# Gated scan and mixture of experts: the router's second layer by column quarters, with new engine orders

## The chip, the cores and the metric

The kernel runs on one core of a Trainium2 chip. The metric is the device time of one execution in microseconds, the median of the timed runs. The profile is of one more execution of the same program, taken by the hardware profiler; times from it are given from the start of its span.

## What is computed

The input is 2 x 2048 tokens of 128 numbers. The first half is a gated linear scan over time, the second a mixture of eight experts, of which each token takes the two best:

```python
h = _layernorm(x, axis=-1) * (1 + ca) + sa
x = x + ga * _L0_attn_ref(h, ...)        # gates, a linear scan along the 2048 tokens
h = _layernorm(x, axis=-1) * (1 + cb) + sb
# the second half, for each token of h:
logits = silu(h @ rw1 + rb1)             # 128 -> 512, the first router layer
logits = logits @ rw2 + rb2              # 512 -> 8, the second router layer
k_logits, k_index = jax.lax.top_k(logits, 2)
k_prob = softmax(k_logits)
# the sum over the two experts e of a token: k_prob * (silu(h @ w1[e] + b1[e]) @ w2[e] + b2[e])
```

All is float32. sa, ca, ga, sb, cb and gb come from a small product of silu(c) with wmod.

## The kernel before, in words

The 4096 tokens are cut into eight groups of 512 (G), four to each sequence. Each group g passes through these parts, and each part is a function in the code, named as in the plan:

- stats1, norm1 (VectorE, L630 to L647) and rstd1 (GpSimd, L450): the first layer norm. turn_x (TensorE, L930), modulate (ScalarE, L525), gates (TensorE, L977 and L978), tanh, decay, clamp, mult (ScalarE, L533 to L553), input (VectorE, L699) and scan (VectorE, L706 and L711): the scan over time, each group after the one before.
- turn_y (TensorE) and resid (VectorE, L716, with the second layer norm's statistics), rstd2 (GpSimd, L475), norm2 (VectorE, L725 and L730), turn_h (TensorE), copy (ScalarE, L559), dup (ScalarE, L563).
- router n (TensorE, L1001): a quarter h of the first router layer for group g, n = 4 g + h. silu n (ScalarE, L572) writes it to SBUF, hidden units on the partitions and 512 tokens along them. It alternates between banks 2 and 3, so router n + 2 waits for silu n.
- logits g (TensorE, L1015): the second router layer, with the activations standing and the eight columns of weights streamed, for each of four token tiles four products that add up in PSUM.
- top2 g (VectorE, L736 to L753) adds the second bias, finds the two best experts and their masks. share g (ScalarE, L577) makes the probabilities. rank g (TensorE, L1024 and L1027) counts the tokens ahead of each in its expert, place g (VectorE, L760 to L769) makes each token's slot.
- send n (GpSimd, L483): four indirect DMAs that write two token tiles, two copies each, to the sorted rows in HBM. There are sixteen sends, 64 DMAs.

After group 3, count:0 and table1 make the table of the first nine expert tiles (EARLY), which SyncE may load (L375) when the first half's dispatches have landed. After group 7, count:1 and table2 make the rest; SyncE first writes padding behind each expert's rows (L364, eight DMAs, which wait for pad_i from table2), then waits for the table, for the padding and for the second half's dispatches, and loads tile 9 onward.

An expert tile s is 256 rows of one expert, 39 tiles in all: tx (turn, L1041), xT (VectorE, L864), l1 (L1052), hid (ScalarE, L585), l2 (L1065), yb (L594), ty (L1073), sc (VectorE, L890), scat (GpSimd, L492, two indirect DMAs), with w1 and w2 (VectorE, L873 and L882) copying the expert's weights. From tile 12 on these run in a loop with a fixed order.

Each engine runs its parts strictly in the order in which its list in PLAN names them, and every part waits on semaphores for what it reads and for the buffers that it overwrites. Of the old lists the parts that matter here are:

```python
"vector": ... norm2:2 top2:0 norm1:6 place:0 input:4 input:5 scan:4 norm2:3 top2:1 stats1:7 place:1 resid:4 scan:5
          ... top2:7 w2:3 sc:1 place:7 xT:5 w1:5 sc:2 w2:4 w2:5 xT:6 w1:6 sc:3 table2:0
"scalar": ... silu:4 dup:0 dup:1 tanh:5 silu:5 copy:2 silu:6 share:0 silu:7 decay:5
"gpsimd": ident:0 rstd1:0 const:0 wsel:0 rstd1:1 ... rstd1:5 rstd2:0 rstd2:1 rstd2:2 rstd1:6
          rstd2:3 send:0 send:1 rstd1:7 send:2 rstd2:4 send:3 rstd2:5 send:4 send:5 rstd2:6 send:6 send:7 rstd2:7 send:8 ...
```

## Time and profile before

| what | value |
|---|---|
| median of 3 timed runs | 314.01 us |
| lowest and highest | 312.12, 314.21 us |
| span of the profiled execution | 344.7 us (the page gives no other time for it) |
| granted TensorE clock, mean over the span | 0.880 |
| TensorE, VectorE, ScalarE, GpSimd busy | 79%, 57%, 50%, 48% |

Times of the profile are of that one execution and run from its first instruction. "PE" is TensorE's products, "PEld" its weight loads, "DVE" VectorE, "ACT" ScalarE, "POOL" GpSimd, "SP" SyncE; a line such as L1015 is a line of the kernel. A float32 product is recorded as two weight loads and two matmuls.

### The profile page before, as it was taken

The page shows a single profiled execution, that of the slowest core. Times are in us where ns is not written, and L with a number is a line of the kernel's source. Part 1 is how long each engine was busy: PE and PEld are TensorE (multiplying, and loading weights), DVE is VectorE, ACT ScalarE, POOL GpSimd, SP SyncE. Part 2 cuts the span into 40 slices and gives each one's busy share as a digit, 9 for nine tenths or more (in the row PEclk, how much of TensorE's full clock was granted, in tenths as well). Part 3 has the DMA queues.
Part 4 walks back from the last instruction along what each step waited for, and adds up shares of the span by engine and source line. Part 5 has one row for each costly group of instructions (what it writes and reads, how often), then busy time and mean ns, then how long its engine had stood idle before and what let it go on. Part 6 is the DMA issues. An engine that isn't in the chain of part 4 may idle for free.

```text
span 344.7 us, 5139 instructions
## 1 busy us (share of the span) xinstructions
PE 273.9 (79%) x1290; PEld 208.6 (61%) x1290; DVE 196.8 (57%) x730; ACT 172.6 (50%) x327; POOL 164.5 (48%) x181
## 2 busy tenths in 40 slices
PE   0877598996978856999934799999999999999400
PEld 0543246664546444868823578888888888888300
DVE  4989899876967643544450234444434444447626
ACT  1079988796867403532400444555555554555100
POOL 4322013378668471547575344544555445555700
PEclk9999698788797876986996699999999999999955
DMA  8990000011111151101122353222222365002366
GB/s 232 321 276 0 0 2 2 8 57 39 40 46 42 54 142 29 33 32 54 42 77 77 92 136 96 70 60 55 62 72 76 84 172 156 19 23 67 92 186 179
DMA packets 41080, 28.43 MB, mean 82 GB/s; under 512 B 4895, under 2 KB 37713, under 8 KB 41056
## 3 DMA queue, kind: packets, MB, share of 16 engines
q1 hardware_dynamic: 34034, 18.60, 20.1%
q0 software_dynamic: 4544, 8.47, 7.5%
q10 hardware_dynamic: 2478, 1.09, 1.2%
q8 instruction: 9, 0.15, 0.2%
q14 instruction: 15, 0.12, 0.1%
HBM read 16.39 MB, written 12.67 MB: 84 GB/s over the span
## 4 chain that ended last, share of the span: by engine, by line
PE 58%; DVE 14%; another core or an unknown queue 9%; ACT 8%; issue 5%; DMA 3%; POOL 1%; DVEq 1%; SPq 0%; POOLq 0%; ACTq 0%
PE bank L1052 20%; PE bank L1065 16%; PE bank L1001 7%; PE bank L1015 4%; PE bank L1041 3%; PE bank L1073 2%; PE bank L977 2%; PE bank L930 2%; PE bank L978 2%; DVE st L630 2%; DMA av<-expert_out 1%; ACT hT L525 1%; ACT hT L585 1%; DVE rows L725 1%
## 5 line engine op out<-in xcount | busy, mean ns | idle before, releaser
L492 POOL DMA_INDIRECT expert_out<-shared,tx x78 | 78.0, 1000 | 73.1 <-DVE shared L890 59.7
L585 ACT ACTIVATE hT<-bank,w_t 128x256 f32<-128x256 f32 x156 | 65.2, 471 | 45.5 <-PE bank L1052 26.1
L483 POOL DMA_INDIRECT sorted_rows<-rows,sloti x64 | 65.3, 1021 | 41.4 <-DVE sloti L769 23.8
L1052 PE MATMUL bank<-xT,w_t 128*128 128x256 f32 x312 | 79.8, 402 | 0.0
L1065 PE MATMUL bank<-hT,w_t 128*128 128x256 f32 x312 | 75.8, 387 | 0.1
L1052 PEld LDWEIGHTS bank<-xT,w_t 128*128 128x128 f32 x312 | 60.8, 204 | 8.9 <-issue 1.2
L1065 PEld LDWEIGHTS bank<-hT,w_t 128*128 128x128 f32 x312 | 57.8, 196 | 6.8 <-DVE w_t L882 0.3
L1001 PE MATMUL bank<-h2T,rw_s 128*128 128x512 f32 x64 | 41.5, 752 | 7.8 <-issue 3.9
L594 ACT ACTIVATE yT<-bank,w_t 128x256 f32<-128x256 f32 x39 | 18.5, 474 | 49.9 <-PE bank L1065 32.0
L864 DVE COPY xT<-bank 128x256 f32<-128x256 f32 x39 | 16.5, 424 | 39.3 <-PE bank L1041 21.8
L873 DVE COPY w_t<-w_s 128x516 f32 x39 | 17.2, 440 | 25.0 <-issue 13.9
L890 DVE TENSOR_TENSOR shared<-bank,tx 128x256 f32<-128x256 f32 x39 | 16.5, 424 | 25.9 <-PE bank L1073 21.6
L1041 PE MATMUL bank<-ident,tx 128*128 128x128 f32 x78 | 15.9, 287 | 14.1 <-DVE xT L864 7.9
L882 DVE COPY w_t<-w_s 128x513 f32 x39 | 17.2, 442 | 15.8 <-issue 12.7
L1073 PE MATMUL bank<-ident,yT 128*128 128x128 f32 x78 | 15.9, 286 | 8.7 <-issue 7.5
L475 POOL TENSOR_TENSOR rs<-ve,half_neg 128x4 f32<-128x4 f32 x8 | 8.7, 1087 | 28.9 <-DVE ve L635 28.8
L1041 PEld LDWEIGHTS bank<-ident,tx 128*128 128x128 f32 x78 | 11.0, 151 | 18.9 <-issue 15.8
L1001 PEld LDWEIGHTS bank<-h2T,rw_s 128*128 128x128 f32 x64 | 12.0, 225 | 13.7 <-issue 5.6
L1073 PEld LDWEIGHTS bank<-ident,yT 128*128 128x128 f32 x78 | 11.0, 147 | 14.8 <-issue 9.5
L977 PE MATMUL bank<-hT,wx_bd 128*128 128x512 f32 x16 | 12.8, 896 | 6.3 <-ACT hT L525 6.3
L450 POOL TENSOR_TENSOR rs<-ve,half_neg 128x4 f32<-128x4 f32 x8 | 8.2, 1026 | 19.0 <-DVE ve L635 19.0
L1015 PEld LDWEIGHTS bank<-rw_s,qv 128*128 128x128 f32 x128 | 15.9, 204 | 1.7 <-issue 1.0
(176 smaller groups left out, 354.6 us busy)
## 6 DMA issues: line engine op xcount, KB each, us to landing
tx<-sorted_rows SPq DMA_DIRECT2D x39, 130.0 KB
w_s<-in_L_ffn_w_dram SPq DMA_DIRECT2D x16, 256.0 KB, 6.2
xs<-in_L_attn_x_dram SPq DMA_DIRECT2D x8, 256.0 KB, 5.2
av<-expert_out SPq DMA_DIRECT2D x8, 256.0 KB, 3.8
qv<-expert_out SPq DMA_DIRECT2D x8, 256.0 KB, 5.4
expert_out<-shared,tx POOLq DMA_INDIRECT x78
sorted_rows<-padr SPq DMA_DIRECT2D x9, 130.0 KB
sorted_rows<-rows,sloti POOLq DMA_INDIRECT x64
```

Source lines behind the costliest of these rows:

```text
L483: p.indirect_dma_start(sorted_rows[:, :], bass.IndirectOffsetOnAxis(ap=sloti[:, k, t:t + 1], axis=0), rows[:, t, k, :], None).then_inc(s_d ...
L492: p.indirect_dma_start(expert_out[:, :], bass.IndirectOffsetOnAxis(ap=xr_i[:, s % U, n, D + 1:D + 2], axis=0), yo[:, s % U, n, :], None, b ...
L585: ins = nc.scalar.activation(hsT[:, u % 2, h, :], bank[4 + q][:, (h % 2) * SL:(h % 2 + 1) * SL], ACT.Silu, bias=w1_t[:, u % 2, HID + h:HID ...
L594: nc.scalar.activation(yT[:, u % 2, :], bank[7][:, 0:SL], ACT.Identity, bias=w2_t[:, u % 2, HC * D:W2E]).then_inc(s_yT_e, 1)
L873: v.tensor_copy(w1_t[:, u % 2, :], w1_s[:, bass.ds(e * WE, WE)]).then_inc(s_w1t, 1)
L977: t.matmul(bank[z][:, :], wx_bd[:, :], hT[:, cols(g)], start=True, stop=True)
L1001: t.matmul(bank[2 + n % 2][:, :], rw1_s[:, h * P:(h + 1) * P], h2T[:, g % 2, :], start=True, stop=True).then_inc(s_rl1, 1)
L1015: ins = t.matmul(bank[6][:, j * NE:(j + 1) * NE], hr[g % 2][:, h, j * P:(j + 1) * P], rw2_s[:, h, :], start=(h == 0), stop=(h == HC - 1))
L1041: ins = t.transpose(bank[1][:, n * P:(n + 1) * P], xr[:, u, n, 0:D], ident[:, :])
L1052: ins = t.matmul(bank[4 + h // 2][:, (h % 2) * SL:(h % 2 + 1) * SL], w1_t[:, u % 2, h * P:(h + 1) * P], xT[:, u % 2, :], start=True, stop= ...
L1065: ins = t.matmul(bank[7][:, 0:SL], w2_t[:, u % 2, h * D:(h + 1) * D], hsT[:, u % 2, h, :], start=(h == 0), stop=(h == HC - 1))
L1073: ins = t.transpose(bank[1][:, n * P:(n + 1) * P], yT[:, u % 2, n * P:(n + 1) * P], ident[:, :])
```

## The change

The second router layer is computed the other way round. The weights stand: for each quarter h of the hidden units, 128 x 32 columns of which eight are used and 24 are zero (rw2_q). The activations are streamed, 512 columns. Each quarter writes its own 32 partitions of bank 6, and nothing is added up in PSUM (logits). A new ScalarE part, lgq, copies the bank to SBUF and adds the second bias, which stands on the first eight partitions (rb2_c). A new TensorE part, fold, multiplies the four token tiles of that copy with a 128 x 8 matrix of four stacked unit matrices (fold), which adds the quarters and turns the result. top2 reads the logits from PSUM; its bias addition goes, and so does the product that spread the bias. The logits, ranks and counts move between banks 6 and 7. VectorE builds the two new constants in consts. All four lists of PLAN are new. In the diff below the old lists are left out.

```diff
+        rw2_q = sb("rw2_q", [P, HC, P // HC])
+        rb2_c = sb("rb2_c", [P, 1])
+        fold = sb("fold", [P, NE])
+        lgq = sb("lgq", [P, G])
...
-        ones_row = sb("ones_row", [1, P])
...
-        lg = sb("lg", [P, GT, NE])
...
-        rb2_row = sb("rb2_row", [1, NE])
-        rb2_b = sb("rb2_b", [P, NE])
...
+        def logit_bank(g):
+            return bank[7 if g < GPB else 6][:, 0:GT * NE]
+
         def rank_bank(g):
-            return bank[7][:, 0:GT * NE] if g < GPB else bank[6][:, GT * NE:2 * GT * NE]
-
-        def counted():
-            return bank[6][:, 2 * GT * NE:2 * GT * NE + NE]
+            return bank[7 if g < GPB else 6][:, GT * NE:2 * GT * NE]
+
+        def counted(n):
+            return bank[7 - n][:, 2 * GT * NE:2 * GT * NE + NE]
...
             "tensor": """
+                turnc:0 turnb:0 mod:0 turn_x:0 gates:0 modrow:0 turn_x:1 turn_x:2 turn_x:3 gates:1 gates:2
+                gates:3 turn_y:0 turn_x:4 turn_x:5 gates:4 turn_h:0 turn_y:1 gates:5 turn_y:2 turn_y:3
+                router:0 router:1 router:2 router:3 turn_h:1 logits:0 router:4 fold:0 turn_x:6 router:5
+                router:6 router:7 turn_h:2 gates:6 rank:0 router:8 router:9 logits:1 turn_h:3 turn_y:4 fold:1
+                router:10 router:11 turn_y:5 router:12 router:13 router:14 rank:1 logits:2 turn_x:7 router:15
+                fold:2 gates:7 turn_y:6 rank:2 logits:3 turn_h:4 fold:3 router:16 router:17 turn_h:5 rank:3
+                router:18 router:19 turn_y:7 count:0 logits:4 router:20 router:21 turn_h:6 fold:4 router:22
+                router:23 router:24 rank:4 turn_h:7 router:25 router:26 logits:5 router:27 fold:5 router:28
+                router:29 router:30 rank:5 router:31 logits:6 tx:0 tx:1 l1:0 fold:6 l1:1 tx:2 l2:0 tx:3 l2:1
+                ty:0 rank:6 l1:2 ty:1 logits:7 tx:4 l1:3 l2:2 tx:5 fold:7 l2:3 l1:4 rank:7 tx:6 l1:5 ty:2
+                count:1 l2:4 l1:6 l2:5 ty:3 ty:4 l2:6 tx:7 tx:8 l1:7 ty:5 l1:8 ty:6 l2:7 tx:9 ty:7 l2:8 tx:10
+                l1:9 ty:8 l1:10 tx:11 l2:9 tx:12 l1:11 ty:9 l2:10""",
             "vector": """
+                stats1:0 setup:0 stats1:1 setup2:0 norm1:0 csilb:0 soft:0 mods:0 stats1:2 stats1:3 colsb:0
+                norm1:1 norm1:2 norm1:3 stats1:4 stats1:5 input:0 scan:0 rowsA:0 norm1:4 norm1:5 resid:0
+                consts:0 input:1 norm2:0 input:2 input:3 scan:1 scan:2 scan:3 resid:1 resid:2 norm2:1 resid:3
+                stats1:6 stats1:7 norm1:6 norm2:2 top2:0 input:4 scan:4 norm2:3 place:0 input:5 input:6 scan:5
+                top2:1 norm1:7 resid:4 resid:5 norm2:4 place:1 scan:6 top2:2 place:2 resid:6 norm2:5 top2:3
+                input:7 scan:7 place:3 resid:7 norm2:6 norm2:7 top2:4 place:4 table1:0 table1b:0 w1:0 w1:1
+                top2:5 place:5 w2:0 xT:0 xT:1 rowsB:0 w1:2 top2:6 xT:2 w2:1 w2:2 xT:3 w1:3 place:6 sc:0 sc:1
+                xT:4 w1:4 w1:5 w2:3 top2:7 xT:5 w2:4 w2:5 xT:6 w1:6 place:7 sc:2 table2:0 w2:6 sc:3 sc:4 w2:7
+                w1:7 xT:7 xT:8 w2:8 w1:8 w1:9 sc:5 sc:6 xT:9 sc:7 w2:9 w1:10 xT:10 sc:8 w2:10 xT:11 w1:11
+                w1:12 xT:12 w2:11 sc:9""",
             "scalar": """
+                ecs:0 esp:0 modulate:0 tanh:0 decay:0 clamp:0 modulate:1 mult:0 modulate:2 modulate:3 tanh:1
+                decay:1 tanh:2 tanh:3 decay:2 decay:3 modulate:4 clamp:1 clamp:2 modulate:5 mult:1 mult:2
+                clamp:3 mult:3 tanh:4 copy:0 decay:4 clamp:4 mult:4 silu:0 silu:1 tanh:5 silu:2 silu:3 copy:1
+                decay:5 lgq:0 clamp:5 silu:4 silu:5 silu:6 modulate:6 dup:0 copy:2 silu:7 tanh:6 silu:8 silu:9
+                dup:1 share:0 mult:5 lgq:1 copy:3 decay:6 silu:10 silu:11 dup:2 silu:12 clamp:6 mult:6 share:1
+                silu:13 silu:14 lgq:2 dup:3 dup:4 modulate:7 silu:15 share:2 tanh:7 decay:7 lgq:3 copy:4
+                clamp:7 mult:7 silu:16 silu:17 share:3 copy:5 silu:18 silu:19 lgq:4 silu:20 silu:21 copy:6
+                silu:22 share:4 silu:23 silu:24 silu:25 silu:26 dup:5 dup:6 copy:7 dup:7 lgq:5 silu:27 silu:28
+                silu:29 share:5 lgq:6 hid:0 hid:1 silu:30 share:6 yb:0 yb:1 silu:31 hid:2 lgq:7 hid:3 yb:2
+                share:7 yb:3 hid:4 hid:5 yb:4 hid:6 yb:5 yb:6 hid:7 hid:8 yb:7 yb:8 hid:9 hid:10 yb:9 hid:11""",
             "gpsimd": """
+                ident:0 const:0 wsel:0 rstd1:0 rstd1:1 rstd1:2 rstd1:3 rstd1:4 rstd1:5 rstd2:0 rstd2:1 rstd2:2
+                rstd1:6 rstd1:7 rstd2:3 send:0 rstd2:4 rstd2:5 send:1 send:2 send:3 send:4 rstd2:6 rstd2:7
+                send:5 send:6 send:7 send:8 send:9 send:10 send:11 send:12 send:13 send:14 send:15 scat:0
+                scat:1 scat:2 scat:3 scat:4 scat:5 scat:6 scat:7 scat:8 scat:9 scat:10 scat:11 scat:12""",
...
...
                 sp.dma_start(xs[:, tiles(g), :], x_t[:, tiles(g), :]).then_inc(s_x[g], 16)
             sp.dma_start(rw1_s[:, :], rw1).then_inc(s_rw, 16)
             sp.dma_start(rw2_s[:, :, :], rw2.rearrange("(c p) e -> p c e", p=P)).then_inc(s_rw, 16)
-            sp.dma_start(rb2_row[:, :], rb2.rearrange("(a e) -> a e", a=1)).then_inc(s_rw, 16)
+            sp.wait_ge(s_zero, 2)
+            sp.dma_start(rb2_c[0:NE, :], rb2.rearrange("(e a) -> e a", a=1)).then_inc(s_rw, 16)
             for g in range(GPB, NG):
                 sp.dma_start(xs[:, tiles(g), :], x_t[:, tiles(g), :]).then_inc(s_x[g], 16)
             for e in range(NE):
...
             def identity(_):
                 p.memset(ident[:, :], 0.0).then_inc(s_zero, 1)
+                p.memset(rb2_c[:, :], 0.0).then_inc(s_zero, 1)
                 p.memset(half_neg[:, :], -0.5).then_inc(s_const, 1)
                 pool.wait_ge(s_const, 1)
                 pool.wait_ge(s_zero, 1)
...
             def constants(_):
                 p.memset(before[:, :], 1.0).then_inc(s_zero, 1)
-                pool.wait_ge(s_zero, 2)
+                pool.wait_ge(s_zero, 3)
                 p.affine_select(out=before[:, :], in_=before[:, :], compare_op=ALU.is_gt, fill=0.0,
                                 base=0, pattern=[[1, P]], channel_multiplier=-1).then_inc(s_const, 1)
                 p.memset(ones_h[:, :], 1.0).then_inc(s_const, 1)
-                p.memset(ones_row[:, :], 1.0).then_inc(s_const, 1)
+                p.memset(rw2_q[:, :, :], 0.0).then_inc(s_const, 1)
                 p.iota(iota_i[:, 0:GT * NE], pattern=[[0, GT], [1, NE]], base=0, channel_multiplier=0)
                 p.iota(iota_i[0:1, 64:64 + LATE], pattern=[[1, LATE]], base=0, channel_multiplier=0)
                 p.iota(iota_i[0:1, 128:128 + LATE], pattern=[[SL, LATE]], base=0, channel_multiplier=0)
...
                     ins = p.iota(rows_i[:, :, k, D + 1], pattern=[[P, NT]], base=k * TOK, channel_multiplier=1)
                 ins.then_inc(s_const, 1)
                 p.memset(padr[:, :, :], 0.0).then_inc(s_zero, 1)
-                pool.wait_ge(s_zero, 3)
+                pool.wait_ge(s_zero, 4)
                 p.iota(padr_i[:, :, D + 1], pattern=[[P, HALVES]], base=TOPK * TOK,
                        channel_multiplier=1).then_inc(s_const, 1)
...
                 act.wait_ge(s_rl1, n + 1)
                 nc.scalar.activation(hr[g % 2][:, h, :], bank[2 + n % 2][:, :], ACT.Silu,
                                      bias=rb1_s[:, h:h + 1]).then_inc(s_hr, 1)
+
+            def gather_logits(g):
+                act.wait_ge(s_lp, g + 1)
+                if g >= 1:
+                    act.wait_ge(s_lg, g)
+                nc.scalar.activation(lgq[:, :], bank[6][:, :], ACT.Identity, bias=rb2_c[:, :]).then_inc(s_lgq, 1)
             def second_share(g):
                 act.wait_ge(s_dlt, g + 1)
...
                                      bias=w2_t[:, u % 2, HC * D:W2E]).then_inc(s_yT_e, 1)
...
             def top2(g):
                 dve.wait_ge(s_lg, g + 1)
-                v.tensor_tensor(lg[:, :, :], bank[6][:, 0:GT * NE].rearrange("p (j e) -> p j e", e=NE),
-                                rb2_b[:, :].unsqueeze(1).to_broadcast([P, GT, NE]), ALU.add).then_inc(s_lgc, 1)
-                dve.wait_ge(s_lgc, g + 1)
+                lg = logit_bank(g).rearrange("p (j e) -> p j e", e=NE)
                 for j in range(GT):
                     ins = v.max(best[:, j, :], lg[:, j, :])
                 link(ins)
                 for j in range(GT):
                     ins = v.max_index(bidx[:, j, :], best[:, j, :], lg[:, j, :])
-                link(ins)
+                ins.then_inc(s_lgc, 1)
+                dve.wait_ge(s_lgc, g + 1)
                 v.tensor_tensor(dlt[:, g % 2, :], best[:, :, 1], best[:, :, 0], ALU.subtract).then_inc(s_dlt, 1)
                 link(v.tensor_copy(bidf[:, :, :], bidx[:, :, 0:TOPK].rearrange("p j k -> p k j")))
                 m = mk[:, g % 2, :, :, :]
...
             def mod_rows(_):
                 dve.wait_ge(s_modb, 1)
-                v.tensor_copy(rb2_b[:, :], bank[6][:, 3 * D:3 * D + NE])
                 for b in range(B):
                     m = bank[6 + b]
                     v.tensor_copy(sbB[:, b, :], m[:, 0:D])
...
                 link(v.memset(val2[:, 1, :], 1.0))
                 v.memset(val2[:, 1, NE - 1:NE], float(1 - NE))
                 v.memset(val2[:, 1, NENT - 1:NENT], 0.0)
+                dve.wait_ge(s_ident, 1)
+                dve.wait_ge(s_rw, 48)
+                link(v.tensor_tensor(fold[:, :], ident[:, 0:NE], ident[:, P // HC:P // HC + NE], ALU.add))
+                for h in range(2, HC):
+                    link(v.tensor_tensor(fold[:, :], fold[:, :], ident[:, h * (P // HC):h * (P // HC) + NE], ALU.add))
+                v.tensor_copy(rw2_q[:, :, 0:NE], rw2_s[:, :, :]).then_inc(s_quart, 1)
                 v.tensor_scalar(mboth[:, 0, 0, :], eid[:, 0, :], float(REG // P), None, ALU.mult)
                 link(v.tensor_scalar(ereg[:, :], eid[0:1, 0, :], float(REG), None, ALU.mult))
...
             def early_table(_):
                 dve.wait_ge(s_cnt, 1)
-                link(v.tensor_tensor(cmpk[:, :, :, :], bank[7][0:1, 0:NE].unsqueeze(2).unsqueeze(3)
+                link(v.tensor_tensor(cmpk[:, :, :, :], counted(0)[0:1, :].unsqueeze(2).unsqueeze(3)
                                      .to_broadcast([1, NE, 2, KT]), kthr[:, :, :, :], ALU.is_gt))
                 link(v.tensor_reduce(full[:, :, :], cmpk[:, :, :, :], AX.X, ALU.add))
                 link(v.tensor_scalar(val1[:, 0, :], full[:, :, 1], -float(SL), float(REG), ALU.mult, ALU.add))
...
             def late_table(_):
                 dve.wait_ge(s_cnt, 2)
-                v.tensor_copy(pad_i[:, :], counted()[0:1, :]).then_inc(s_pads, 1)
-                link(v.tensor_tensor(cmpk[:, :, 0, :], counted()[0:1, :].unsqueeze(2).to_broadcast([1, NE, KT]),
+                v.tensor_copy(pad_i[:, :], counted(1)[0:1, :]).then_inc(s_pads, 1)
+                link(v.tensor_tensor(cmpk[:, :, 0, :], counted(1)[0:1, :].unsqueeze(2).to_broadcast([1, NE, KT]),
                                      kthr[:, :, 0, :], ALU.is_gt))
                 link(v.tensor_reduce(nent[:, NE:NENT], cmpk[:, :, 0, :], AX.X, ALU.add))
                 link(v.tensor_tensor(nent[:, NE:NENT], nent[:, NE:NENT], full[:, :, 0], ALU.subtract))
...
                 for b in range(B):
                     ins = t.matmul(bank[6 + b][:, 0:3 * D], csil_b[:, b, :], wmod_s[:, 3 * D:6 * D],
                                    start=True, stop=True)
-                pe.wait_ge(s_rw, 48)
-                pe.wait_ge(s_const, 5)
-                ins = t.matmul(bank[6][:, 3 * D:3 * D + NE], ones_row[:, :], rb2_row[:, :], start=True, stop=True)
                 ins.then_inc(s_modb, 1)
             def xn_transpose(g):
...
                 if g == 0:
                     pe.wait_ge(s_modrow, 1)
+                    pe.wait_ge(s_quart, 1)
                 else:
-                    pe.wait_ge(s_lgc, g)
-                if g > GPB:
+                    pe.wait_ge(s_lgq, g)
+                    if g > GPB:
+                        pe.wait_ge(s_slot, g)
+                for h in range(HC):
+                    part = slice(h * (P // HC), (h + 1) * (P // HC))
+                    ins = t.matmul(bank[6][part, :], rw2_q[:, h, :], hr[g % 2][:, h, :], start=True, stop=True)
+                ins.then_inc(s_lp, 1)
+
+            def fold_logits(g):
+                pe.wait_ge(s_lgq, g + 1)
+                if g >= 1:
                     pe.wait_ge(s_slot, g)
                 for j in range(GT):
-                    for h in range(HC):
-                        ins = t.matmul(bank[6][:, j * NE:(j + 1) * NE], hr[g % 2][:, h, j * P:(j + 1) * P],
-                                       rw2_s[:, h, :], start=(h == 0), stop=(h == HC - 1))
+                    ins = t.matmul(logit_bank(g)[:, j * NE:(j + 1) * NE], lgq[:, j * P:(j + 1) * P], fold[:, :],
+                                   start=True, stop=True)
                 ins.then_inc(s_lg, 1)
             def ranks(g):
...
             def count(n):
                 pe.wait_ge(s_slot, (n + 1) * GPB)
-                to = bank[7][:, 0:NE] if n == 0 else counted()
-                t.matmul(to, ones_h[:, :], mboth[:, (n + 1) * GPB, 0, :], start=True, stop=True).then_inc(s_cnt, 1)
+                t.matmul(counted(n), ones_h[:, :], mboth[:, (n + 1) * GPB, 0, :], start=True, stop=True).then_inc(s_cnt, 1)
             def turn_rows(s, u):
                 pe.wait_ge(s_xr[u], 16 * rounds(s, u))
...
```

## Rows read from the trace of the kernel before

**Rows 1.** The page: busy time of each engine, and the shares of the chain.
```profile
PE 273.9 (79%) x1290; PEld 208.6 (61%) x1290; DVE 196.8 (57%) x730; ACT 172.6 (50%) x327; POOL 164.5 (48%) x181
...
PE 58%; DVE 14%; another core or an unknown queue 9%; ACT 8%; issue 5%; DMA 3%; POOL 1%; DVEq 1%; SPq 0%; POOLq 0%; ACTq 0%
PE bank L1052 20%; PE bank L1065 16%; PE bank L1001 7%; PE bank L1015 4%; PE bank L1041 3%; PE bank L1073 2%; PE bank L977 2%; PE bank L930 2%; PE bank L978 2%; DVE st L630 2%; DMA av<-expert_out 1%; ACT hT L525 1%; ACT hT L585 1%; DVE rows L725 1%
```

**Rows 2.** The chain in order of time: start us, length us, what.
```profile
65.31 0.86 PE bank L1001 x2
66.17 3.47 PE bank L1015 x32
...
110.93 5.05 another core or an unknown queue
...
124.80 7.29 another core or an unknown queue
...
172.48 7.08 another core or an unknown queue
179.60 9.88 another core or an unknown queue
...
219.46 1.73 PE bank L1052 x8
...
223.35 1.73 PE bank L1052 x8
```

**Rows 3.** Busy time of the engines in two stretches, with the granted clock.
```profile
core 0: us, PE busy (x) PEld busy (x) DVE busy (x) ACT busy (x) POOL busy (x), PEclk, DMA share, GB/s
...
40.00:60.00 20.00, 17.81 (x76) 10.25 (x75) 18.77 (x88) 17.99 (x26) 4.53 (x4) 0.84 0.01 2
60.00:80.00 20.00, 20.00 (x106) 13.56 (x104) 16.35 (x77) 16.80 (x25) 12.30 (x11) 0.82 0.10 31
```

**Rows 4.** Timeline of GpSimd: start us, length us, operation, idle before it.
```profile
64.89 1.36 POOL L483 DMA_INDIRECT sorted_rows<-rows,sloti  x1 [6.89 <-DVE sloti L769]
...
140.60 0.95 POOL L483 DMA_INDIRECT sorted_rows<-rows,sloti  x1 [9.91 <-DVE sloti L769]
...
174.24 0.96 POOL L483 DMA_INDIRECT sorted_rows<-rows,sloti  x1 [0.30 <-issue]
175.51 1.28 POOL L483 DMA_INDIRECT sorted_rows<-rows,sloti  x1 [0.30 <-issue]
```

**Rows 5.** Timeline of SyncE's DMA issues.
```profile
175.24 18.25 SPq L364 DMA_DIRECT2D sorted_rows<-padr  x8
196.23 76.60 SPq L375 DMA_DIRECT2D tx<-sorted_rows  x27
```

**Rows 6.** Timeline of TensorE where tile 9 is turned.
```profile
201.91 0.36 PEld L1041 LDWEIGHTS bank<-ident,tx 128*128 128x128 f32 x2
```

**Rows 7.** Groups by line and shape: out<-in xcount | busy us, mean ns of one.
```profile
L1015 PE MATMUL bank<-rw_s,av 128*128 128x8 f32 x128 | 14.7, 255 | 0.0
...
L475 POOL TENSOR_TENSOR rs<-ve,half_neg 128x4 f32<-128x4 f32 x8 | 8.7, 1087 | 28.9 <-DVE ve L635 28.8
...
L559 ACT COPY h2T<-bank 128x512 f32<-128x512 f32 x8 | 4.7, 582 | 18.3 <-remote 16.8 <-PE bank L930 1.5
...
L736 DVE TENSOR_TENSOR lg<-bank,rb_b 128x32 f32<-128x32 f32 x8 | 1.5, 187 | 7.6 <-remote 6.1 <-PE bank L1015 1.5
```

**Rows 8.** The same view: VectorE's larger groups of the first stage.
```profile
L630 DVE BATCH_NORM_STATS2 st<-xs 128x6 f32<-128x128 f32 x64 | 13.9, 280 | 3.8 <-DMA xs<-in_L_attn_x_dram 3.5
...
L730 DVE SCALAR_TENSOR_TENSOR rows<-rows,rs,sbB 128x128 f32<-128x128 f32 x32 | 9.2, 348 | 0.3
L725 DVE SCALAR_TENSOR_TENSOR rows<-xs,mv,cbB 128x128 f32<-128x128 f32 x32 | 9.0, 343 | 0.1
...
L711 DVE TENSOR_TENSOR_SCAN hT<-av,hT,tx 128x512 f32<-128x512 f32 x6 | 7.7, 1284 | 0.2
...
L706 DVE SCALAR_TENSOR_TENSOR tx<-tx,gac,qv 128x512 f32<-128x512 f32 x8 | 6.0, 748 | 2.2 <-ACT qv L553 2.2
...
L699 DVE SCALAR_TENSOR_TENSOR tx<-tx,hT 128x512 f32<-128x512 f32 x8 | 5.4, 684 | 0.7 <-ACT shared L534 0.6
```

41 lines of the change are left out of this document (4 added, 37 removed).

## The prediction

> **What bounds the kernel now.** I read the page first. TensorE is the busiest engine (273.9 of 344.7 us) and more than half of the chain that ended last is its work, the expert layers (L1052, L1065) ahead of everything else; the second router layer, L1015, the code that the change replaces, has 4% of it [rows 1]. The same row gives 9% of the chain to "another core or an unknown queue". I then read the chain in order of time. It has four long pieces of that kind, at 110.93, 124.80, 172.48 and 179.60 us, together 5.05 + 7.29 + 7.08 + 9.88 = 29.3 us [rows 2]: work had been issued and its completion came late, and no instruction of the kernel stands in them. The profiled execution's span is 344.7 us and the median of the timed runs 314.01 us, 30.7 us less. The page gives no other time for that execution. I take it that these pieces are the difference: 344.7 x 8.7% = 30.0 us (the sum of all such pieces), and 344.7 - 30.0 = 314.7 us. So I argue in "cleared" time, a trace time less the pieces before it, and set it against 314.0 us.
>
> The chain has three stages. From the start to the first dispatch at 64.89 us the VectorE and the ScalarE are the full engines: 18.77 and 17.99 of the 20 us from 40 to 60 [rows 3]. From there to the load of tile 9 the GpSimd queue counts: 64 dispatch DMAs, one every 1.27 us (174.24 to 175.51), back to back except where the group's slots are late, 9.91 us once, most of it one of the four pieces [rows 4]. SyncE loads tile 9 at 196.23 us, after the eight padding writes that begin at 175.24 [rows 5]: cleared, 196.23 - 30.0 = 166.2 us. The dispatches end about 176.8 us, cleared of the first two pieces 176.8 - 12.3 = 164.5 us. So padding and dispatch end within 2 us of each other. The third stage is TensorE alone: 30 tiles, one in 223.35 - 219.46 = 3.89 us [rows 2]. Nothing of the change is in it. From the load of tile 9 to the end it is 344.7 - 196.2 = 148.5 us, and what the change can give it must give before that load, or in how ready TensorE is when the tile lands (it turned tile 9 at 201.91 [rows 6], 5.7 us after the load was issued).
>
> **TensorE's part of the change.** Removed, in each of eight groups: 16 products of 8 columns, recorded as 32 weight loads and 32 products, 3.47 us in the chain at 66.17 [rows 2], that is 0.108 us for a pair; the records alone are 255 ns each, as they overlap [rows 7]. Added, first: four quarter products of 512 streamed columns. No row shows one with 32 weight columns. The nearest is the first router layer, 128x512, two records of 0.43 us = 0.86 us at the full clock (65.31 [rows 2]). If all four run side by side: 0.86 us. If one waits for the other: 4 x 0.86 = 3.44 us. As each product is two records on the same quarter, a third way lies between: the second record of one beside the first of the next, 5 x 0.43 = 2.1 us. I take 2.1 us; both ends stay in the range. Added, second: the fold, four products of 8 columns, eight pairs x 0.108 = 0.87 us. Sum: 2.1 + 0.87 = 3.0 us for 3.47 us, 0.5 us less a group; bounds 1.73 us (1.7 less) and 4.31 us (0.8 more); for eight groups 4 us less, from 14 less to 7 more. The small product for the second bias goes (one, under 0.6 us, once, early and beside other work).
>
> The Trainium skill, "TensorE: Matmul & The Clock Gate", part 3 (packing small matmuls), says that matmuls in different column groups run concurrently and start some 4 ns apart, and gives 2.38 times for three tiles; by it the four quarters would take about the 0.86 us of one. No row here shows two products side by side. "TensorEngine Tiling (Array Packing)", Key Properties, speaks the other way: changing the tiling mode drains TensorE, and this change switches mode twice in each group. Neither gives a term of the sum.
>
> **ScalarE and VectorE.** ScalarE gets eight copies of 128x512 out of PSUM; the router copy L559 is the nearest, 582 ns [rows 7], so 8 x 0.58 = 4.7 us. In the first stage they come on a full engine [rows 3]; later they are beside free time. And they lengthen each group's way to its ranks: quarters, copy, fold where there was one step. 3.0 + 0.6 = 3.6 us against 3.47 us: nothing, if the copy isn't queued behind something. What is queued behind it is silu, which frees the banks for the next router products. The VectorE loses the bias addition L736 (187 ns plus its wait, 0.2 us a group) and gets five small operations once (about 1 us by that row), since the maxima now read PSUM. The bias column's DMA waits on SyncE for two fills by GpSimd that start the kernel, with the later input loads queued behind it; at most a few tenths, hidden by the first group's work.
>
> A new wait: fold g waits for the slots of group g - 1. Behind it on TensorE stand router products; the rank product had that wait already, a few steps later.
>
> **The orders.** This is the larger part. In the old order VectorE does top2:0, norm1:6, place:0. The new one has stats1:7, input:4, scan:4 and norm2:3 ahead of place:0 as well. By [rows 8]: statistics 4 x 0.28 and what belongs to them, 1.5 us; input 0.68; scan 0.75 + 1.28 = 2.0; norm2 4 x 0.343 + 4 x 0.348, overlapped, 2.3; together 6.5 us, with the five small ones 7.5, less 0.2. VectorE has no free time there, so the first dispatch moves from 64.9 to about 72 us. ScalarE agrees: share:0, which place:0 waits for, now stands behind dup:1, silu:9 and tanh:6.
>
> Then GpSimd's own order: send:0 (4 DMAs, 5.1 us, to 77), rstd2:4, rstd2:5, then send:1. rstd2:5 needs resid:5, and VectorE has, from place:0 (about 71) on, place 1, two inputs 1.4, scan 2.0, top2 2.1, norm1 1.1, two resid 4.4 (addition and statistics; place, top2 and norm1 are my estimates from how closely their small operations of 0.16 to 0.4 us follow each other in the trace): 12 us, so 83; two powers and send:1 starts at 85. GpSimd waits some 6 us. Send:1 to send:4 are 16 x 1.27 = 20.3 us, to 105. Next it wants resid:7: VectorE has norm2:4, norm2:5 4.6, place 1 to 3 3.0, scan 6 and 7 4.0, top2 2 and 3 4.2, input 0.7, resid 6 and 7 4.4: 21 us from 83, thus 104, with small waits 106; send:5 starts at 108. Then 44 x 1.27 = 55.9 us: 164. With about 2 us for the last to land, tile 9 can be loaded at 166, where it was 166.2. After place:7 the padding comes quicker than before: count:1 and table2 now stand right behind it, where VectorE had three weights and three tiles between; this takes padding off the end and leaves the dispatch there. So the cleared load of tile 9 doesn't move, and from it the same 148.5 us would follow: 166 + 148.5 = 314.5 us. Off that I take 2.5 us, since TensorE comes to tile 9 with 4 us less behind it and more of the early tiles done, and turned tile 9 later than the load allowed: 312.0 us.
>
> **The rivals.** A: TensorE, not the dispatch, sets tile 9, and the quarters run side by side. For it: TensorE was busy all 20 us from 60 to 80 [rows 3]. Against it: GpSimd's dispatches have few gaps of their own. Price: the full 1.74 x 8 = 14 us, held by GpSimd: with the first dispatch at 68 and no waits, 68 + 64 x 1.27 + 5 powers of 1.1 (L475 [rows 7]) = 155, landed at 157, 9 us before 166: 314 - 9 = 305 us.
>
> B, the other side: the dispatch is what ends last and the new order starves it. Place: GpSimd between send:0 and send:1, and before send:5, where rstd2:5 and rstd2:7 now stand ahead of tokens that have their slots. Price: from 85 us on every us that resid:5 is later goes straight to the end; VectorE at 85% instead of full makes its 12 and 21 us into 14 and 25, and the first dispatch 74: 2 + 2 + 4 = 8 us: 320 us. It decides as soon as send:5 starts after 111.
>
> C: the change doesn't do what it says: the quarters run one after another. 0.84 us more a group at the full clock; at the half level, which the mean of 0.82 from 60 to 80 [rows 3] shows to be present, twice that. With four to five groups on the path, 5 us: 317 us.
>
> **How the numbers follow.** A measurement of this kernel tells about 1% (3.1 us) from no change. My forecast 0.45, with 308 to 316 as its own range; A 0.22; B 0.23; C 0.10. Faster: A and 0.12 of the forecast, 0.34. Slower: B's 0.22 and half of C, 0.27. Within 1%: 0.39. The range goes to 304 for A with all of its saving and to 321 for B.
>
> **What would show it.** First L483 near 72 us; between send:0 and send:1 an idle of some 6 us put down to L635; 3.0 us from the first quarter product to the fold's end without the copy; the load of tile 9 at a cleared 166 us; the same 3.89 us a tile. I am wrong if the first dispatch stays at 65, if the four quarters take 0.9 us or 3.4 us and the load of tile 9 moves with them, or if the four pieces without an owner are in the timed runs too.

## The result, and the profile of the changed kernel

The changed kernel takes 316.27 us (median of 12 runs, 313.31 to 318.79), the kernel before 313.85 us beside it (12 runs, 311.65 to 315.91). The ratio is 1.0069, 95% interval 1.0041 to 1.0097: 0.7% slower. That is less than the 1% that the prediction took for measurable, but the interval leaves out no change. The forecast was 312.0 us, on the other side. The ratios leave out executions more than 1.5% above the fastest of their kernel: the profiled one of the change is among them, five of the ten of e3 (whose fastest took 310.77 us), and one of the kernel before beside e15 that took 926.45 us.

The profiled execution of the changed kernel took 318.79 us, the longest of the twelve; its span is 316.9 us. In all runs of the change the span is 1.8 to 1.9 us shorter than the time (1.7 to 2.2 over all kernels), which the prediction didn't know. For comparison the kernel before was profiled again (the first experiment): 312.11 us, span 310.2. I call it "before again".

The page of the changed kernel, busy time and the chain that ended last, which answers to [rows 1]:

```profile
PE 252.6 (80%) x1160; PEld 182.7 (58%) x1160; DVE 195.7 (62%) x725; ACT 177.9 (56%) x335; POOL 163.8 (52%) x182
...
PE 52%; ACT 15%; POOL 9%; DVE 8%; issue 7%; DMA 5%; SPq 1%; DVEq 1%; POOLq 0%; ACTq 0%
```

And the busy time of before again:

```profile
PE 264.3 (85%) x1290; PEld 203.8 (66%) x1290; DVE 196.1 (63%) x730; ACT 172.7 (56%) x327; POOL 165.3 (53%) x181
```

TensorE is busy 11.7 us less (264.3 - 252.6), more than the 4 us that was forecast, and the kernel is slower. Nothing without an owner is in the chain.

The new layer, in the groups by line and shape (mean ns of one behind the comma), with the copy (the old layer's row is in [rows 7], 14.7 us):

```profile
L1039 PE MATMUL bank<-fold,lgq 128*128 128x8 f32 x64 | 10.2, 287 | 7.4 <-ACT lgq L587 7.4
...
L1031 PE MATMUL bank<-qv,rw_q 128*32 128x512 f32 x32 | 4.3, 604 | 0.0
...
L587 ACT ACTIVATE lgq<-bank,rb_c 128x512 f32<-128x512 f32 x8 | 5.4, 680 | 4.0 <-PE bank L1031 4.0
```

The fold is the dearer part: 10.2 us of products of eight columns against 2 x 4.3 = 8.6 us for all the quarter products (half of them read av, with a row like this one), and TensorE waits 7.4 us in all for the copy ahead of it.

The timeline of GpSimd, the rows with a wait over 1 us from the first dispatch to the last (in brackets the idle time before the row), which answers to [rows 4]:

```profile
69.75 1.36 POOL L491 DMA_INDIRECT sorted_rows<-rows,sloti  x1 [10.18 <-DVE sloti L782]
78.33 1.04 POOL L483 TENSOR_TENSOR rs<-ve,half_neg 128x4 f32<-128x4 f32 x1 [3.43 <-DVE ve L649]
80.44 1.04 POOL L483 TENSOR_TENSOR rs<-ve,half_neg 128x4 f32<-128x4 f32 x1 [1.07 <-DVE ve L649]
106.74 1.04 POOL L483 TENSOR_TENSOR rs<-ve,half_neg 128x4 f32<-128x4 f32 x1 [1.94 <-DVE ve L649]
107.96 1.04 POOL L491 DMA_INDIRECT sorted_rows<-rows,sloti  x1 [0.18 <-issue]
...
145.48 0.96 POOL L491 DMA_INDIRECT sorted_rows<-rows,sloti  x1 [2.03 <-DVE sloti L782]
...
158.54 0.96 POOL L491 DMA_INDIRECT sorted_rows<-rows,sloti  x1 [3.27 <-DVE sloti L782]
...
167.85 0.95 POOL L491 DMA_INDIRECT sorted_rows<-rows,sloti  x1 [0.30 <-issue]
```

The same rows of before again (two more of its waits are 1.83 and 0.87 us):

```profile
63.54 1.36 POOL L483 DMA_INDIRECT sorted_rows<-rows,sloti  x1 [6.88 <-DVE sloti L769]
...
125.07 0.95 POOL L483 DMA_INDIRECT sorted_rows<-rows,sloti  x1 [3.37 <-DVE sloti L769]
...
157.18 0.96 POOL L483 DMA_INDIRECT sorted_rows<-rows,sloti  x1 [0.30 <-issue]
```

Up to 107.96 the changed kernel does what the prediction says: first dispatch at 69.75 (72 was said), send:5 at 107.96 (108 was said). Then come two waits, 2.03 and 3.27 us, for the slots of groups 6 and 7, which weren't forecast. Before again has group 7's slots at 147.61, where the change has them at 158.54.

SyncE's issues, of the changed kernel and then of before again ([rows 5]):

```profile
126.23 10.23 SPq L382 DMA_DIRECT2D tx<-sorted_rows  x9
159.47 8.58 SPq L371 DMA_DIRECT2D sorted_rows<-padr  x8
171.47 73.55 SPq L382 DMA_DIRECT2D tx<-sorted_rows  x27
```

```profile
112.93 9.94 SPq L375 DMA_DIRECT2D tx<-sorted_rows  x9
153.93 8.46 SPq L364 DMA_DIRECT2D sorted_rows<-padr  x8
165.07 34.72 SPq L375 DMA_DIRECT2D tx<-sorted_rows  x17
```

Tile 0 can be loaded 13.3 us later than before, tile 9 6.4 us later. From the load of tile 9 to the end of the span it is 316.9 - 171.47 = 145.4 us here and 310.2 - 165.07 = 145.1 us before. So in these two executions the whole difference stands ahead of tile 9, and nothing behind it was won.

Where TensorE's 11.7 us went is seen in the views by stretch up to the turn of tile 9 (columns as in [rows 3]), first the changed kernel (tile 9 turned at 174.50), then before again (167.83):

```profile
0.00:112.90 112.90, 79.18 (x293) 40.68 (x293) 94.54 (x439) 84.28 (x122) 46.61 (x64) 0.88 0.26 78
112.90:128.00 15.10, 10.92 (x53) 4.20 (x52) 8.86 (x49) 7.63 (x14) 11.44 (x13) 1.00 0.20 61
128.00:167.80 39.80, 36.19 (x173) 29.56 (x173) 21.83 (x86) 17.19 (x40) 26.63 (x28) 0.87 0.35 97
167.80:174.50 6.70, 6.14 (x31) 5.17 (x32) 2.77 (x7) 3.36 (x8) 5.12 (x6) 1.00 0.39 111
```

```profile
0.00:112.90 112.90, 91.49 (x396) 56.23 (x396) 96.92 (x451) 83.66 (x120) 56.18 (x72) 0.86 0.28 83
112.90:128.00 15.10, 14.60 (x85) 12.23 (x84) 9.42 (x48) 7.04 (x16) 9.10 (x10) 0.89 0.51 125
128.00:167.80 39.80, 37.96 (x201) 32.09 (x202) 22.14 (x87) 16.57 (x40) 28.88 (x30) 0.91 0.26 80
```

The changed kernel's TensorE is busy 79.18 + 10.92 + 36.19 + 6.14 = 132.4 of 174.5 us before tile 9's turn, the old one's 144.1 of 167.8: the 11.7 us are all there, as idle time (42.1 us for 23.7). From the turn it is 142.4 us to the end in both (316.9 - 174.50, 310.2 - 167.83). A tile of the loop takes 3.90 us in the chain, as before.

It is not the load of tile 9 that TensorE was waiting for there. In both executions it turned the tile with no idle time before it, 3.03 and 2.76 us after the load was issued, where the pages give 2.2 us for such a load to land. The chain that ended last passes elsewhere. These are three of its pieces in the change, then in before again:

```profile
158.66 0.06 DVE pad_i L858
...
163.08 0.19 DVE tab L871
...
174.66 0.23 PE bank L1064 x2
```

```profile
153.12 0.06 DVE pad_i L840
...
157.50 0.19 DVE tab L853
...
167.99 0.23 PE bank L1041 x2
```

pad_i and tab are the start and the end of table2 on VectorE. table2 needs the slots of group 7 and releases the padding; behind it the chain runs over VectorE's copies and TensorE's last early tiles to the turn of tile 9.

### The profile page after: what moved, and what is told of

Read it like the earlier page. It is cut to its first block, busy times and chain, and to the rows that moved or that the text cites. A ratio compares the mean times of both kernels' runs of the same rounds, so it can differ in the third digit from the quotient of the medians.

```text
span 316.9 us, 4896 instructions
## 1 busy us (share of the span) xinstructions
PE 252.6 (80%) x1160; PEld 182.7 (58%) x1160; DVE 195.7 (62%) x725; ACT 177.9 (56%) x335; POOL 163.8 (52%) x182
## 4 chain that ended last, share of the span: by engine, by line
PE 52%; ACT 15%; POOL 9%; DVE 8%; issue 7%; DMA 5%; SPq 1%; DVEq 1%; POOLq 0%; ACTq 0%
PE bank L1075 20%; PE bank L1088 18%; POOL sorted_rows L491 7%; PE bank L1016 3%; PE bank L1064 3%; PE bank L1096 3%; PE bank L992 2%; ACT L561 2%; ACT hT L533 2%; DMA av<-expert_out 2%; DMA wa_c<-in_L_attn_w_a_dram 1%; PE bank L993 1%; PE bank L1039 1%; ACT qv L556 1%; ACT qv L551 1%
## 5 line engine op out<-in xcount | busy, mean ns | idle before, releaser
L1075 PE MATMUL bank<-xT,w_t 128*128 128x256 f32 x312 | 77.7, 394 | 0.1
L1088 PE MATMUL bank<-hT,w_t 128*128 128x256 f32 x312 | 74.1, 380 | 0.4 <-ACT yT L608 0.4
L1075 PEld LDWEIGHTS bank<-xT,w_t 128*128 128x128 f32 x312 | 58.7, 198 | 7.5 <-DVE w_t L891 0.4
L1088 PEld LDWEIGHTS bank<-hT,w_t 128*128 128x128 f32 x312 | 56.5, 191 | 6.8 <-issue 0.6
L1016 PE MATMUL bank<-h2T,rw_s 128*128 128x512 f32 x64 | 36.5, 689 | 4.9 <-ACT qv L580 3.5
L992 PE MATMUL bank<-hT,wx_bd 128*128 128x512 f32 x16 | 11.6, 818 | 7.4 <-ACT hT L533 5.1
L644 DVE BATCH_NORM_STATS2 st<-xs 128x6 f32<-128x128 f32 x64 | 13.9, 280 | 5.6 <-DMA xs<-in_L_attn_x_dram 5.3
L1096 PE MATMUL bank<-ident,yT 128*128 128x128 f32 x78 | 15.1, 275 | 2.8 <-ACT yT L608 1.1
L1039 PEld LDWEIGHTS bank<-fold,lgq 128*128 128x128 f32 x64 | 10.3, 239 | 10.8 <-ACT lgq L587 10.2
```

Of the source, the lines that this page charges most:

```text
L992: t.matmul(bank[z][:, :], wx_bd[:, :], hT[:, cols(g)], start=True, stop=True)
L1016: t.matmul(bank[2 + n % 2][:, :], rw1_s[:, h * P:(h + 1) * P], h2T[:, g % 2, :], start=True, stop=True).then_inc(s_rl1, 1)
L1075: ins = t.matmul(bank[4 + h // 2][:, (h % 2) * SL:(h % 2 + 1) * SL], w1_t[:, u % 2, h * P:(h + 1) * P], xT[:, u % 2, :], start=True, stop= ...
L1088: ins = t.matmul(bank[7][:, 0:SL], w2_t[:, u % 2, h * D:(h + 1) * D], hsT[:, u % 2, h, :], start=(h == 0), stop=(h == HC - 1))
L1096: ins = t.transpose(bank[1][:, n * P:(n + 1) * P], yT[:, u % 2, n * P:(n + 1) * P], ident[:, :])
```

## The experiments

Fifteen runs. "Tile 9" is the start of its load, "rest" the time from there to the end of the span, "padding" its first write, "turn" TensorE's turn of tile 9; these and the first dispatch are of each kernel's one profiled execution. Ratios are to the kernel before, run on the same chip beside it.

| kernel | median us | ratio, 95% interval | first dispatch | padding | tile 9 | rest | turn |
|---|---|---|---|---|---|---|---|
| before again | 312.11 (one) | | 63.54 | 153.93 | 165.07 | 145.1 | 167.83 |
| the change | 316.27 | 1.0069, 1.0041 to 1.0097 | 69.75 | 159.47 | 171.47 | 145.4 | 174.50 |
| e2 old layer, new orders | 324.47 | 1.0291, 1.0220 to 1.0363 | 71.36 | 164.99 | 178.78 | 146.6 | 181.41 |
| e3 new layer, old orders | 315.21 | 1.0008, 0.9960 to 1.0057 | 65.32 | 158.30 | 169.86 | 145.4 | 172.25 |
| e4 ranks before tiles | 321.62 | 1.0262, 1.0223 to 1.0302 | 72.43 | 154.77 | 167.88 | 151.9 | 176.80 |
| e5 GpSimd's order | 317.12 | 1.0103, 1.0041 to 1.0166 | 68.67 | 156.39 | 169.28 | 144.7 | 171.71 |
| e6 ranks before tiles, 2 | 320.45 | 1.0193, 1.0168 to 1.0217 | 71.73 | 161.33 | 173.18 | 145.5 | 176.37 |
| e7 one column group | 317.66 | 1.0110, 1.0086 to 1.0135 | 69.18 | 157.83 | 170.59 | 145.0 | 172.92 |
| e8 e5 and e6 | 322.34 | 1.0251, 1.0222 to 1.0279 | 71.54 | 165.63 | 177.56 | 145.0 | 180.65 |
| e9 old head, new tail | 319.70 | 1.0179, 1.0145 to 1.0213 | 63.64 | 159.69 | 171.50 | 146.2 | 174.72 |
| e10 new head, old tail | 319.06 | 1.0148, 1.0097 to 1.0198 | 70.03 | 160.53 | 171.63 | 145.6 | 174.45 |
| e11 dispatch delayed | 322.18 | 1.0242, 1.0198 to 1.0285 | 68.95 | 154.58 | 171.14 | 147.7 | 173.54 |
| e12 TensorE kept at work | 316.02 | 1.0050, 1.0019 to 1.0081 | 69.65 | 155.33 | 168.02 | 145.2 | 170.33 |
| e13 fold:6 first | 316.50 | 1.0069, 1.0017 to 1.0122 | 71.36 | 157.03 | 169.53 | 145.2 | 172.03 |
| e14 e12 and e13 | 317.10 | 1.0081, 1.0055 to 1.0108 | 72.03 | 161.57 | 174.04 | 145.3 | 176.60 |
| e15 new layer, old orders, 2 | 314.48 | 1.0055, 1.0018 to 1.0093 | 62.73 | 154.68 | 165.98 | 145.5 | 168.61 |

The stretches are read first. The rest is 144.7 to 146.6 us in all but two rows (e4, e11). The turn of tile 9 is the closer measure: from it to the end it is 142.0 to 143.1 us in all rows but e2 (144.0) and e11 (145.3). And the turn stands at a fixed distance behind the first padding write, which starts with table2: 13.9 to 14.0 us where the last part of the lists is the old one (before again, e3, e10, e15), 15.0 to 15.3 where it is new, except e2 (16.4), e4 (22.0) and e11 (19.0). For the load of tile 9 TensorE waits 1.65 us in e2 and 4.27 us in e11 (at its weight load), 0.2 to 0.5 us in e5, e7 and e12, and not at all in the other eleven. The chains of the change, before again, e12, e13 and e15 all pass through pad_i. So in most of these executions the start of table2 gives the time, and the load lands just before TensorE comes. The places differ between executions of one kernel by several us (the first dispatch is 68.7 to 72.4 under the same lists ahead of it), so the verdicts go by the ratios, and the places say only by which way.

**e1, the kernel before, profiled again.** No edit.

> The kernel before, unchanged, profiled once more. My reading: the four chain pieces without an owner (29.3 us) belong to that one profiled execution; without them the span is 311 to 314 us, the first dispatch stands at 63 to 66 us, the first tile load near 112, the load of tile 9 at 165 to 168. Rival: they belong to the kernel, and the span is again above 340 us.

Span 310.2 us, no piece without an owner in the chain. The 30 us of [rows 2] were of that one execution. The load of tile 9 is at 165.07 where the prediction had worked out 166.2. One thing differs from the picture that the prediction drew: the last dispatch is over at 157.18 + 0.96 = 158.1 us, the padding's last issue at 153.93 + 8.46 = 162.4 us, 2.7 us before the load. Even if the dispatch takes 3.2 us to land (e13, below) it is there at 161.3. So before the change the padding released the load of tile 9, and the dispatch had some 3.8 us of slack to it.

**e2 and e3, the two halves of the change.** e2 is the old layer with the new lists, e3 the new layer with the old ones.

```diff
 # e2: the kernel before, all four lists of the change, without
-  lgq:0 ... lgq:7   fold:0 ... fold:7
 # e3: the change, all four old lists, with each fold two parts behind its logits, and
+  silu:4 lgq:0 ... silu:8 lgq:1 ... mult:5 lgq:2 ... mult:6 lgq:3 ... silu:20 lgq:4 ... silu:26 lgq:5 ... silu:29 lgq:6 ... yb:1 lgq:7
```

> The kernel before with the four new orders, lgq and fold left out: only the orders change. Theory (the orders cost, the new layer gives): slower than the changed kernel, 318 to 323 us, since each group has 3.47 us of TensorE work again for 1.9 us, and the late dispatch stays. Rival (the new layer with its copy is what costs): 314 us or less, below the changed kernel.

> The changed kernel with the old orders; lgq and fold are put in two or so parts behind logits. Theory (the layer gives 1.5 us of TensorE time a group, the orders take it away): first dispatch at 64 to 67 us, load of tile 9 a few us earlier than in the changed kernel, 308 to 313 us. Rival (three steps instead of one lengthen every group's way to its slots): 316 us or more.

The new orders with the old layer cost 2.9%, some 9 us. Under them the new layer gives back 2.9 - 0.7 = 2.2%, 7 us. Under the old orders it gives nothing, although TensorE's busy time falls to 252.8 us there too. The 1.0008 is that of five executions; all ten have a median of 315.21 us for 313.78, and e15, the same but for three neighbours, has 1.0055. These intervals overlap the change's, so what part of its 0.7% belongs to the orders isn't shown. e2's waits for the slots of groups 6 and 7 are larger than the change's, 4.17 and 7.10 us.

**e4, e6: the ranks of groups 6 and 7 ahead of the first tiles.** In the new lists fold:6 stands behind tx:0, tx:1 and l1:0 on TensorE, top2:6 behind xT:0 and xT:1 on VectorE. Group 6's moves are shown; both kernels also move logits, fold, top2, rank and place of group 7 up, e4 further than e6 and with count:1.

```diff
 # tensor
-  logits:6 tx:0 tx:1 l1:0 fold:6 l1:1 tx:2 l2:0 tx:3 l2:1 ty:0 rank:6
+  logits:6 fold:6 tx:0 tx:1 l1:0 rank:6 l1:1 tx:2 l2:0 ...
 # vector; e4 moves table2:0 ahead of w2:4 besides, e6 leaves it
-  w2:0 xT:0 xT:1 rowsB:0 w1:2 top2:6 xT:2 w2:1 w2:2 xT:3 w1:3 place:6
+  w2:0 top2:6 xT:0 xT:1 place:6 rowsB:0 w1:2 xT:2 ...
 # scalar
-  lgq:6 hid:0 hid:1 silu:30 share:6 yb:0 yb:1 silu:31
+  lgq:6 silu:30 share:6 silu:31 hid:0 hid:1 yb:0 ...
```

> The changed kernel with only the end of the router reordered: fold 6, top2 6, share 6, rank 6 and place 6 no longer stand behind the first expert tiles, and group 7 follows directly. Theory (TensorE waits 4.5 us for tile 0 with fold 6 queued behind it, so the slots of groups 6 and 7 come late and GpSimd idles 2.0 and 3.3 us): these two waits go, the dispatch ends 5 us earlier, 311 to 313 us. Rival (padding or TensorE's tiles end last there anyway): within 1 us of the changed kernel, 315 to 317 us.

> The changed kernel with fold 6, top2 6, share 6, rank 6 and place 6 ahead of the first expert tiles, as in e4, but with VectorE's weights, tiles and table2 where the changed kernel has them: in e4 GpSimd's waits went and tile 9 was loaded at 167.9 us, yet from there to the end it was 151.9 us, not the 145.3 of e1 and of the changed kernel. Theory (e4's early tiles were starved by VectorE's order, nothing else): load of tile 9 at 167 to 168 us and 145 to 146 us behind it, 313 to 314.5 us. Rival (groups 6 and 7 ahead of the tiles cost TensorE as much as the waits did): 316 us or more.

In e4 GpSimd's two waits are gone and tile 9 is loaded at 167.88, 3.6 us earlier, and it is 1.9% slower than the change: the rest takes 151.9 us. The early tiles are late, TensorE is busy only 33.4 us of the 40 from 130 to 170 (37.5 in the change), and it turns tile 9 at 176.80, 8.9 us after the load was issued. In e6, with the table where it was, the rest is 145.5 again, but a wait of 2.11 us for group 7 stays and the padding is at 161.33. So two things must be there for tile 9, the sorted rows and a TensorE that is through with the early tiles, and in both kernels the second comes later than in the change: turned at 176.80 and 176.37, for 174.50.

**e5, e8: GpSimd's own order.**

```diff
-  send:0 rstd2:4 rstd2:5 send:1 send:2 send:3 send:4 rstd2:6 rstd2:7 send:5 send:6 send:7
+  send:0 send:1 rstd2:4 rstd2:5 send:2 send:3 send:4 rstd2:6 send:5 send:6 rstd2:7 send:7
```

> The changed kernel with only GpSimd's list changed: send 1 before the powers rstd2 4 and 5, send 5 and 6 before rstd2 6 and 7. Theory (GpSimd's waits of 3.4 + 1.1 us before send 1 and 1.9 us before send 5 go straight to the end, as my prediction had it): the first half's dispatch ends 2 to 4 us earlier, tile 9 is loaded 2 to 3 us earlier, 313 to 314.5 us. Rival (the slots of groups 6 and 7 come late anyway, so the gain turns into a longer wait for them): first tile load earlier, tile 9 unchanged within 1 us, 315.5 to 317 us.

> e5 and e6 together. Theory: with the slots of groups 6 and 7 on time, GpSimd's earlier sends do reach the end: tile 9 loaded at 164 to 166 us, 310 to 312.5 us, below both kernels. Rival (TensorE's own work from tile 0 on sets the end as soon as the dispatch doesn't): as e6, 313 to 314.5 us, with more than 146 us behind the load of tile 9.

e5 loads tile 0 5 us earlier (121.12) and is no faster. On its timeline the time saved at the powers comes back as waits for slots, 2.67, 0.61, 2.06, 2.47 and 3.25 us at 83.60, 117.92, 129.77, 142.40 and 155.45.

e8, the edits of e5 and e6 together, was a miss: the wait for group 7 grows to 9.21 us and the kernel is at 1.0251, slower than e6 (1.0193) and as slow as e4.

**e7, the quarters one after another.** All four into one column group, added up in PSUM; lgq and fold then use these 32 partitions alone:

```diff
+                part = slice(0, P // HC)
...
-                    part = slice(h * (P // HC), (h + 1) * (P // HC))
-                    ins = t.matmul(bank[6][part, :], rw2_q[:, h, :], hr[g % 2][:, h, :], start=True, stop=True)
+                    ins = t.matmul(bank[6][part, :], rw2_q[:, h, :], hr[g % 2][:, h, :], start=(h == 0),
+                                   stop=(h == HC - 1))
...
```

> The changed kernel with the four quarter products in the first 32 columns of the array, added up in the first 32 partitions of the bank; lgq and fold use these 32 partitions alone, the result is the same. Theory (the four quarters take 1.0 us because they run side by side in different column groups): they now take 4 x 0.86 = 3.4 us a group, and the kernel is 3 to 8 us slower than the changed one, 319 to 324 us. Rival (a product with 32 weight columns is short by itself): still about 1 us a group, 316 us.

One group of the change, then one of e7, on TensorE's timeline (x8: two records for each of four products):

```profile
146.40 1.06 PE L1031 MATMUL bank<-qv,rw_q 128*32 128x512 f32 x8
```

```profile
141.93 3.62 PE L1031 MATMUL bank<-qv,rw_q 128*32 128x512 f32 x8
```

1.06 us against 3.62: in four column groups the quarters run side by side, at the price of a single one. That is 2.6 us a group, 20 us in all, and it is worth 1.0110 against 1.0069, 0.4% or 1.3 us, with intervals that overlap. TensorE's busy time is up by only 10.8 us (263.4 for 252.6), at a higher granted clock (0.952 for 0.914, mean over the span). The rest fits into time in which TensorE waited.

**e9, e10: which half of the orders.** The lists of e3 up to the first dispatch and those of the change behind it (e9), and the reverse (e10).

```diff
 # cut behind tensor rank:0, vector place:0, scalar share:0, gpsimd send:0
 # e9: e3's list up to the cut, then what is left in the order of the change
 # e10: the change's list up to the cut, then what is left in e3's order
```

> The new second layer; each engine's list is that of the third experiment (the old orders) up to the first dispatch (tensor to rank:0, vector to place:0, scalar to share:0, gpsimd to send:0) and from there on the new order. Theory (the late first dispatch and the waits between the first groups cost the time, and the rest of the new order is as good as the old): first dispatch at 65 us, 4.4 us earlier than in the changed kernel, tile 9 loaded at 167 to 168, 312 to 313 us. Rival (the waits for the last groups' slots belong to the tail of the new order and take back whatever the head gives): tile 9 at 170 to 171, 315 to 316 us.

> The other way round: the new order up to the first dispatch, the old orders from there on. Theory: first dispatch at 70 us, and as GpSimd's old list has few waits behind it, tile 9 at 169 to 171, 315 to 317 us. Rival (the tail is what costs): as the third experiment or better in the tail, tile 9 at 165 to 167, 311 to 313 us.

Both theories fall: either mixture, 1.0179 and 1.0148, is slower than either whole. e9 dispatches early and then stands 12.01 us before rstd2:4. A mixture has a seam that neither whole has, so it can't say which half of the new orders holds a loss. It does say that an early first dispatch (63.64) is not enough.

**e11, the dispatch alone made later.**

```diff
+                if n == 15:
+                    for i in range(5):
+                        p.tensor_tensor(spare[:, i, :], ve2[:, tiles(7)], half_neg[:, :], ALU.pow)
```

> The changed kernel with five more powers on GpSimd just ahead of send:15, the last dispatch: 5 x 1.04 = 5.2 us and nothing else. Theory (the end of the dispatches alone sets the load of tile 9, and the time follows it one for one): tile 9 at 176.5 to 177, and 321 to 322 us. Rival (TensorE has early tiles of its own left when the dispatches end, so that a later load is partly hidden): tile 9 as late as that, but the time only 318 to 319 us.

1.0242 for 1.0069: 1.7%, 5.4 us for the 4.95 us that the powers took. That looks like one for one, but the trace divides it otherwise. Here TensorE does wait for tile 9:

```profile
173.54 0.69 PE L1068 MATMUL bank<-ident,tx 128*128 128x128 f32 x2 [3.87 <-DMA tx<-sorted_rows]
```

Without this wait it would have turned the tile at 169.67, 15.1 us behind the padding as in the other rows. So about 1 us of the 4.95 was hidden, and the dispatch alone had that much slack to TensorE. Behind the wait the granted clock was 0.53 from 173.5 to 180 us (1.00 in the change from its turn, 174.50 to 181), and from the turn to the end it took 145.3 us for 142.4: 2.9 us more. The profiled execution shows more: it has no wait at the slots of groups 6 and 7, though the lists are the same, and without the delay its dispatches would have ended at about 169.0 - 4.9 = 164.1 us, where the prediction has 164. A difference to the execution shown first is on TensorE. First that of the change, then e11's:

```profile
128.53 0.44 PE L1064 MATMUL bank<-ident,tx 128*128 128x128 f32 x2 [3.36 <-DMA tx<-sorted_rows]
130.10 0.69 PE L1064 MATMUL bank<-ident,tx 128*128 128x128 f32 x2 [1.14 <-DMA tx<-sorted_rows]
130.59 3.62 PE L1075 MATMUL bank<-xT,w_t 128*128 128x256 f32 x8
134.00 1.72 PE L1039 MATMUL bank<-fold,lgq 128*128 128x8 f32 x8
135.57 3.76 PE L1075 MATMUL bank<-xT,w_t 128*128 128x256 f32 x8
```

```profile
126.81 0.44 PE L1068 MATMUL bank<-ident,tx 128*128 128x128 f32 x2 [2.52 <-DMA tx<-sorted_rows]
128.11 0.44 PE L1068 MATMUL bank<-ident,tx 128*128 128x128 f32 x2 [0.86 <-DMA tx<-sorted_rows]
128.38 3.54 PE L1079 MATMUL bank<-xT,w_t 128*128 128x256 f32 x8
131.71 1.04 PE L1043 MATMUL bank<-fold,lgq 128*128 128x8 f32 x8
132.60 1.97 PE L1079 MATMUL bank<-xT,w_t 128*128 128x256 f32 x8
```

TensorE waits 4.5 us for tiles 0 and 1 in the first, 3.4 in the second. That the longer wait decides it is argued, not shown. Behind the longer wait two groups of L1075 and fold:6 take twice their time, behind the shorter one just one group.

**e12, e13, e14: that clock, and fold:6.**

```diff
 # e12, in turn_rows; the result is overwritten by the turn
+                if static(s) and s <= 1:
+                    wait_tile_bank(pe, "tx", s)
+                    for n in range(4 - 3 * s):
+                        t.matmul(bank[1][:, :], ident[:, :], rw1_s[:, :], start=True, stop=True)
 # e13, tensor only
-  logits:6 tx:0 tx:1 l1:0 fold:6
+  logits:6 fold:6 tx:0 tx:1 l1:0
```

> The changed kernel; ahead of the first tile's turn TensorE does four products of 512 columns whose result is overwritten, and one ahead of the second tile's (4 x 0.86 and 0.86 us), in the wait for the first tile load. Theory (the 3.4 and 1.1 us in which TensorE waits for tiles 0 and 1 are followed by the half clock, under which the fold of group 6 and the first products of tiles 0 and 1 take twice as long, and this makes the slots of groups 6 and 7 late): the products of L1075 at 130 to 139 us take 1.9 us and not 3.6, fold:6 0.8 to 1.0 us and not 1.7, GpSimd's waits for the slots of groups 6 and 7 shrink from 5.3 us to under 2, tile 9 is loaded near 168, 312 to 314 us. Rival (the clock of those few us is nothing, the lateness is the order's): waits and tile 9 as before, 316 to 317 us; were the added products on the path, 318 to 320.

> The changed kernel with fold:6 moved on TensorE from behind l1:0 to ahead of tx:0, all other lists as they are. Theory (fold:6 is late because it stands behind a tile that isn't there): fold:6 at 126 us and not at 134, slots of group 6 two to four us earlier, limited by VectorE's xT:0 and xT:1 ahead of top2:6; 314 to 315 us. Rival (VectorE's order holds top2:6, and the half clock stays): 316 to 317 us.

> Both edits together. Theory: with fold:6 ahead and the clock kept full the waits for the slots of groups 6 and 7 go, 311 to 313 us. Rival (each only moves the wait to the next group): no better than the better of the two alone.

In e12's execution the mechanism is as expected: TensorE works through the wait, the products behind it run at full speed, GpSimd has no wait at the slots of groups 6 and 7, padding is 4 us earlier and tile 9 at 168.02.

```profile
125.21 3.70 PE L1064 MATMUL bank<-rw_s,ident 128*128 128x512 f32 x8
...
130.83 1.89 PE L1079 MATMUL bank<-xT,w_t 128*128 128x256 f32 x8
132.56 0.95 PE L1039 MATMUL bank<-fold,lgq 128*128 128x8 f32 x8
133.36 1.98 PE L1079 MATMUL bank<-xT,w_t 128*128 128x256 f32 x8
```

But the median is 316.02 us, against 312 to 314 expected. The interval, 1.0019 to 1.0081, covers the change's 1.0069. Taking the fall of the clock away doesn't move the ratio measurably; how often the change's other executions have it isn't shown. The one of 318.79 us has three slow groups, e11's has one, and e13's two groups of L1075 take 5.24 us together. e13 gave nothing and e14 nothing more; in e14's execution a wait of 3.27 us for the slots of group 7 is left. e13's execution, 316.50 us and so near the change's median, has no waits at the slots of groups 6 and 7 either. Its rows on GpSimd (send:5 and the last dispatch) and on SyncE are used below:

```profile
109.93 1.04 POOL L491 DMA_INDIRECT sorted_rows<-rows,sloti  x1 [0.18 <-issue]
...
165.36 0.96 POOL L491 DMA_INDIRECT sorted_rows<-rows,sloti  x1 [0.30 <-issue]
```

```profile
169.53 30.09 SPq L382 DMA_DIRECT2D tx<-sorted_rows  x15
```

**e15, a better place for the folds in the old orders.**

```diff
-  logits:0 router:5 fold:0 ... logits:2 router:12 fold:2 ... silu:4 lgq:0
+  logits:0 fold:0 router:5 ... logits:2 fold:2 router:12 ... lgq:0 silu:4
```

> The third experiment (new layer, old orders) with three neighbours exchanged: fold:0 ahead of router:5, fold:2 ahead of router:12 on TensorE, and lgq:0 ahead of silu:4 on ScalarE. In the third one TensorE waited 2.25 and 3.68 us in these two router products with the fold queued behind, VectorE waited 2.46 and 5.78 us for those folds, and GpSimd 4.41 us at rstd2:6. Theory (place of the folds in the order, not the layer, kept the new layer from its gain): GpSimd's wait of 4.41 falls to under 1 us, first dispatch 1 to 2 us earlier, tile 9 near 166, 311 to 313 us, ratio to before 0.990 to 0.997. Rival (TensorE's own arrival at tile 9, or the next wait of the dispatches, stands behind it): 314 to 316 us, ratio 1.0.

GpSimd's wait stayed, 4.22 us, and the ratio is 1.0055, on the rival's side. No kernel with the new layer beat the old one.

## Why the prediction was wrong

**Cleared time: right, with an offset.** The four ownerless pieces were not the kernel's, and the tile 9 of an undisturbed execution was met within 1.1 us. But the cleared 314.7 us was compared with the 314.0 us of the timed runs as if both were times; a span is 1.9 us under its time, so the sum was about 2.6 us too long for a span of 312.1 (314.0 - 1.9). That error hid in "the same 148.5 us": measured it is 145.1, and 147.0 with the offset.

**"Off that I take 2.5 us": the step that gave the wrong sign.** It supposed that TensorE came to tile 9 later than the load allowed, read from 5.7 us between load and turn [rows 5, 6]. That row was of the disturbed execution. Before again has 167.83 - 165.07 = 2.76 us, and the page of the changed kernel gives 2.2 us for such a load to land. There were 0.6 us to be had, not 2.5; after the change it is 174.50 - 171.47 = 3.03 us. Nor did TensorE come earlier for having less to do: it turned tile 9 at 174.50 in the change and at 172.03 in e13, for 167.83. The rest, 145.1 before and 145.4, 145.2 and 145.2 after (the change, e12, e13), gave nothing. Without this term the prediction would have said 314.5 us, no change.

**"This takes padding off the end and leaves the dispatch there": the path that failed.** The sum follows the dispatch alone to the load of tile 9. In the profiled executions of the change, e12 and e13 TensorE turned tile 9 15.0 us behind the first padding write and, but for 0.23 us in e12, without a wait for the load. What counted was table2, which waits for the slots of group 7, and the sum took these to be in time. In spans, before again and e13: padding 153.93 and 157.03, +3.1 us; from there to the turn 13.90 and 15.00, +1.1; from the turn to the end 142.4 and 142.7, +0.3. Together that is 4.5 us, 314.7 - 310.2. The new orders put table2 right behind place:7, but group 7's slots came later by more than that gave: 158.54 for 147.61 in the change. Why they come later isn't shown by one experiment. In the change tile 0 is loaded 13.3 us later, and the last folds stand among the early tiles; but e5, with tile 0 5 us earlier, is no faster, and e6, with the folds ahead of the tiles, is slower.

**"44 x 1.27 = 55.9 us: 164": a miss of 2 to 5 us on its own path.** The chain up to it held: the first dispatch moved by 6.2 us, the wait before send:1 was 3.43 + 1.07 = 4.5 us (6 was said), send:5 came at 107.96. In e13, which takes the change's median, send:5 comes at 109.93, the last dispatch is over at 166.3 and tile 9 at 169.53; in e12 it is 164.6 and 168.02. That is 2.0 to 3.5 us over the 166 that was forecast: 1.2 to 1.4 us of it is the landing (3.2 and 3.4 us from the last issue's end, where 2 was taken), the other part of e13's is send:5, held by 3.63 us of waiting ahead of rstd2:7. In the profiled execution of the change the waits for groups 6 and 7 bring it to 171.47, though it dispatches first 1.6 us earlier than e13.

By the prediction's own terms, forecast and e13: 166 + 148.5 - 2.5 = 312.0, and 169.5 + 147.1 - 0 = 316.6 (timed: 316.50), where 147.1 is 145.2 and the offset of 1.9. The three differences are +3.5, -1.4 and +2.5 us; the middle one hid part of the miss, by chance.

**What was late before.** The prediction set padding and dispatch within 2 us of each other. They were 3.8 us apart, the padding last (e1). The new orders do speed the padding, as it said: 159.47 - 158.54 = 0.9 us behind the last group's slots, where it was 153.93 - 147.61 = 6.3. But they start the dispatch 6 us later, with as many us of dispatch behind it (94.6 us from first to last before, 95.0 in e12 and e13). The slack of 3.8 us took part of the 6, and the dispatch now ends with the padding, at 168.80 and 168.05 us, about 1 us before it would hold TensorE up (e11).

**The new layer: 3.0 us a group forecast for 3.47, some 2 us measured.** The quarters took 1.06 us, not 2.1: the bound of 0.86 us was the nearer one. The 14 us of rival A were nearer to the busy time taken off (11.7 us) than the forecast's 4. The Trainium skill, "TensorE: Matmul & The Clock Gate", part 3, says that matmuls in different column groups run concurrently; the trace agrees, 1.06 us for four where one group of columns took 3.62 (e7). The drain at a change of tiling mode, of which the Trainium skill speaks in "TensorEngine Tiling (Array Packing)", Key Properties, can't be seen apart in these rows. The copy takes 680 ns, not 582, and TensorE waits 7.4 us in all for it. But the work taken off, 11.7 us (the change) or 11.5 (e3), became idle time under either set of orders, and 20 us put on (e7) cost 1.3. The forecast had turned 2.5 of its 4 us into time.

**The rivals.** In the profiles of the change, e12 and e13 A was right that TensorE and not the dispatch is last at tile 9, and wrong in the price: when TensorE comes depends on table2 and the early tiles, and 11.7 us less work didn't bring it earlier. B had the right place in part and the wrong price: the starving waits, 4.5 and 1.9 us, were foreseen in the forecast itself, send:5 was not after 111 in the change's trace, and moving the powers (e5) gave nothing. C fell at 1.0 us a group. What it became is a small loss over later slots of group 7. The later first dispatch isn't enough to explain it: e15 dispatches first at 62.73 and is at 1.0055 all the same. No experiment singles out one list or one wait, and what of the new orders makes up e2's 2.9% stays open too.

**The measurement.** The text took 1% for its grain. With twelve runs on each side it tells 0.3%, so "within 1%" had room for both signs.

## What to carry to other kernels

Before a term is taken from how long an engine takes after its data is issued, take it from an undisturbed execution, or compare it with the landing time of that DMA: only what is left over can be won. Where two streams meet at one point (here the sorted rows and the early tiles at tile 9), look first whether the engine waited there or came late itself, and by a deliberate delay of each (e7, e11) measure the slack. Read the delay's trace too: part of its cost here was the slower clock behind the wait. A cheaper operation that adds a hop over another engine should be priced by the wait for that engine, not by its own records.

## What the runs showed of the hardware

TensorE's granted clock fell to its lower level (1.2 GHz) behind a wait of a few us and was still there after work had come back: in the change, after 3.36 and 1.14 us of waiting, it was 0.50 from 130.6 to 139.3 us, and two groups of L1075 took 3.62 and 3.76 us where 1.9 is the rule, and fold:6 1.72 us for 0.95. In e12, kept at work, none did, and the mean granted clock from 128 to 167.8 us was 1.00 for 0.87.

A wait is not needed for it. In before again the three slow groups of L1052 each follow a group of the old layer's eight-column products, with 0.51 us of waiting at most in between. One such pair:

```profile
126.14 3.63 PE L1015 MATMUL bank<-rw_s,av 128*128 128x8 f32 x32
...
130.90 3.42 PE L1052 MATMUL bank<-xT,w_t 128*128 128x256 f32 x8
```

The granted clock was 1.00 from 126.1 to 129.6 us, while L1015 ran, and 0.53 from 130.9 to 134.2; with the third (137.2 to 140.7, 141.0 to 144.3) it was 1.00 and 0.51. e2, with the same layer, has 1.00 from 130.3 to 133.8 us and 0.57 from 135.3 to 138.5. So a part of the 11.7 us is this: 3.4 us for 1.9, three times. That the eight-column products are the reason is argued from their place, not tested.

In e7, which gives TensorE the most to do of the kernels with the new layer, the mean over the span was 0.952 for 0.914 in the change.

Eight records of 604 ns each (four float32 products of 32 x 512, 64 records a kernel) fit into 1.06 us when they write four column groups, so a sum of the records' means counts such work more than four times.
